# Gate stage: VectorE picks the two best experts of a chunk ahead of the low halves of the rows of the next one

## The reference

```python
logits = xf @ gate_w.T
topk_logits, topk_idx = jax.lax.top_k(logits, 2)
topk_w = jax.nn.softmax(topk_logits, axis=-1)
...
shared = jax.nn.silu(xf @ sg_gate.T) * (xf @ sg_up.T) @ sg_down.T
return shared + out
```

## Time and profile before

| | us |
|---|---|
| median of 3 timed runs | 2417.37 (2417.35 to 2419.74) |
| the profiled execution, its own time | 2425.1 |
| its span, first to last instruction | 2423.4 |
| VectorE busy in the span | 1776.7 |
| TensorE matmuls busy in the span | 2185.1 |

### The profile page before, as it was taken

One profiled execution on the slowest core, in us unless ns is written; L12 is line 12 of the kernel. 1 busy time (PEld: TensorE's weight loads), 2 busy tenths in 40 slices (PEclk: granted clock), 3 DMA queues, 4 the chain that ended last, 5 costly groups with the idle time before them and its releaser, 6 DMA issues. The chain is left out here.

```text
span 2423.4 us, 85735 instructions
## 1 busy us (share of the span) xinstructions
PE 2185.1 (90%) x31693; PEld 1375.4 (57%) x31693; DVE 1776.7 (73%) x5603; ACT 1664.1 (69%) x3894; POOL 1076.6 (44%) x1374
## 2 busy tenths in 40 slices
PE   6979999999967788879999995996999999999766
PEld 4643444444435676768888884563455555555354
DVE  5538999999838677744454444984999999999298
ACT  6955899899843555424454443893799999999644
POOL 3533666666654566636666664562000000000076
PEclk9987999999979899989999998997899999999888
DMA  6552333333232566745553344874232222322242
GB/s 220 203 189 75 93 91 94 94 94 93 65 97 87 146 181 185 171 115 128 141 139 96 93 89 127 267 274 147 65 80 79 81 75 81 82 74 69 64 155 95
DMA packets 363746, 290.45 MB, mean 120 GB/s; under 512 B 228400, under 2 KB 296752, under 8 KB 363344
## 3 DMA queue, kind: packets, MB, share of 16 engines
q1 hardware_dynamic: 349616, 248.24, 37.0%
q0 software_dynamic: 12960, 35.60, 4.7%
q10 hardware_dynamic: 768, 1.12, 0.2%
HBM read 133.53 MB, written 123.69 MB: 106 GB/s over the span
## 5 line engine op out<-in xcount | busy, mean ns | idle before, releaser
L765 ACT ACTIVATE a_pr<-a_pst 128x384 f32<-128x384 f32 (+3 forms) x2176 | 909.2, 486 | 112.6 <-PE a_pst L804 87.3
L804 PE MATMUL a_psc<-a_ke,a_qe 52*64 52x192 f16 (+4 forms) x6144 | 632.4, 286 | 32.5 <-DMA a_ke<-mrow 29.7
L804 PE MATMUL a_pst<-a_qe,a_ke 49*64 49x384 f16 (+5 forms) x6144 | 579.4, 288 | 1.6 <-ACT a_pr L765 0.5
L717 DVE TENSOR_REDUCE a_mx<-a_psc 128x1 f32<-128x320 f32 (+1 forms) x1152 | 537.9, 528 | 44.7 <-PE a_psc L804 36.8
L866 PE MATMUL a_po<-a_pr,a_ve 128*17 128x128 f32 (+3 forms) x10496 | 563.5, 303 | 2.0 <-ACT a_pr L765 1.1
L712 DVE CUSTOM_DVE_ANT_0 a_cut<-a_psc,row_mask 128x320 bf16<-128x320 f32 (+1 forms) x1024 | 436.3, 472 | 51.8 <-PE a_psc L804 29.6
L804 PEld LDWEIGHTS a_pst<-a_qe,a_ke 53*64 53x64 f16 (+1 forms) x6144 | 241.3, 105 | 327.9 <-ACT a_pr L765 193.9
L683 POOL TENSOR_SCALAR_AFFINE_SELECT a_pr<-a_pr 128x512 f32<-128x512 f32 x448 | 276.2, 637 | 159.4 <-ACT a_pr L765 159.4
L804 PEld LDWEIGHTS a_psc<-a_ke,a_qe 52*64 52x64 f16 (+1 forms) x6144 | 262.8, 106 | 112.1 <-DVE a_mx L717 36.3
L866 PEld LDWEIGHTS a_po<-a_pr,a_ve 128*17 128x17 f32 x10496 | 193.9, 96 | 181.9 <-issue 50.5
L663 POOL TENSOR_SCALAR a_mneg<-a_mx 128x32 f16<-128x32 f32 x64 | 18.6, 290 | 626.9 <-DVE a_mx L721 584.7
(11 more groups left out here) (242 smaller groups left out, 4168.6 us busy)
## 6 DMA issues: line engine op xcount, KB each, us to landing
a_qe<-qx SPq DMA_DIRECT2D x378, 64.0 KB, 2.7
a_ke<-kx SPq DMA_DIRECT2D x378, 64.0 KB, 2.7
vx<-p_vst SPq DMA_DIRECT2D x32, 544.0 KB, 3.3
a_ve<-vx SPq DMA_DIRECT2D x64, 272.0 KB, 3.0
qx<-p_stg SPq DMA_DIRECT2D x64, 256.0 KB, 3.4
kx<-p_stg SPq DMA_DIRECT2D x64, 256.0 KB, 3.3
ox<-a_ost SPq DMA_DIRECT2D x256, 64.0 KB
x_res<-x SPq DMA_DIRECT2D x16, 512.0 KB, 8.9
```

The lines of the kernel that those rows point to most:

```text
L717: dve.tensor_reduce(out.unsqueeze(1), psc[(u * n_s + n) % RING][:, 0:width], AXX, ALU.max)\
L765: act.activation(pr[s % SLOTS][:, h // 2, h % 2, 0:width], pst[prob_slot(u, n) % RING][:, 0:width], ACT.Exp, scale=scale).then_inc(p_ready, 1)
L804: last = pe.matmul(out[at, col:col + count], stat[:, t * P + 64 * half:t * P + 64 * half + 64], mov[:, tok:tok + count], start=(k == 0), s ...
```

## The change

In VectorE's queue of the gate stage, `top2(s+1)` is issued ahead of `row_lo(s+2)` in each iteration. In the last iteration but one there is no `row_lo`; in the last, `table_of_tiles` stands in the place of `top2`, and there is no `row_lo` either. Nothing else differs.

```diff
                 if s > 0:
                     add_y(s - 1, 1)
                 low(s, 0)
-                if s + 2 < NC:
-                    row_lo(s + 2)
                 if s + 1 < NC:
                     top2(s + 1)
                 else:
                     table_of_tiles()
+                if s + 2 < NC:
+                    row_lo(s + 2)
                 hidden(s, 1)
```

## The result

The changed kernel ran at a median of 2398.07 us (2395.67 to 2402.32, 4 runs), the kernel before on the same chip at 2418.34 us (2417.35 to 2419.74, 4 runs): a ratio of 0.9918, with a 95% interval of 0.9904 to 0.9932. Measured again on another chip, the ratio was 0.9911 (0.9894 to 0.9929). The number was right; the step of the working that gave it, the loop that sets the pace, was not.

The account below looks back on a forecast made before the run. VectorE's wait for ScalarE bounded the 15.84 us pace; afterwards the loop through the transposes would, at 14.3 us. Saving 17 us over 11 iterations plus about 1.5 in iteration 0, taken as 18 off 2417.4, gave 2399 us; range 2386 to 2417.

Parts of the forecast that it names:

- The hole (2.35 us): VectorE's wait before `row_lo` for ScalarE's L1300; `top2` (2.64 us) was to fit there, making all behind 2.35 us early.
- The delay behind the gates: In profiled iteration 14, gate completion reached VectorE 2.3 us after the last matmul began; assumed absent from timed runs.
- no change: Rival: delay behind the gates real in timed runs, transposes 8 us; pace 15.3 us, about 2414 us; chance 0.18.
- slower: Rival: delay behind the gates real, transposes 9.1 us; transpose loop 16.4 us against 15.84, total 2428 us; chance 0.10.
- The pace of 14.3 us from the loop through the transposes: Forecast case: gates, `top2`, `row_lo`, transposes (9.1 us), next gates set iterations 1 to 11 at 14.3 us; chance 0.44.
- the signs named ahead: Steady gates waiting for transposes, new wait before L1356, pace near 14.3 us; no DMA wait would mean transposes mis-sized.
- VectorE's own loop at 13.5 us: Rival: transposes 8 us or below, VectorE sets the pace, 15.84 less 2.35; 2388 or 2382 us; chance 0.20.
- Iterations 12 and 13: Gate-stage iterations without weight halves, already at 14.1 us with a wait for transposes; predicted to win nothing.
- The sum of 18 us: Predicted total gain: 17 us from iterations 1 to 11 and about 1.5 us from iteration 0.
- GpSimd's wait for slots: GpSimd's wait per iteration for VectorE's slots; predicted to fall from 3.2 to under 2 us.
- The rule on shared ports: VectorE instructions with two SBUF inputs and GpSimd's SBUF readers exclude each other; by it `row_lo` would take 1.23 us.

## Why the prediction was right or wrong

**The hole (2.35 us).** Right. `row_lo` stands right behind `top2`, without a wait for L1300. In the old order with block 0 on VectorE the instructions of an iteration take less time, and VectorE still waits there (1.38 or 2.02 us), so that the hole was a matter of order.

**The delay behind the gates.** The choice to put it down to the recording was right: a second profile of the unchanged kernel, and both profiles of the changed one, don't have it. Where VectorE does wait for the gates in the second profile of the changed kernel, `top2` starts 0.20 us after the last of them began (983.71):

```profile
983.91 0.19 DVE L1356 TENSOR_SCALAR g_logit<-g_small 128x32 f32<-128x32 f32 x1 [0.37 <-PE g_small L71]
```

The rivals "no change" and "slower" both hung on it, and fell with it.

**The pace of 14.3 us from the loop through the transposes.** This is the step that failed, though it came within 0.1 us of the measured 14.20. The loop is real, as the runs with extra transposes show, but it was mis-sized. Its main term was 9.1 us for the transposes, where at most 7.5 are measured at 891.89 to 899.36, 7.2 to 7.9 in the three chunks of the changed kernel whose gates waited, and 6.5 to 8.5 in the run with one transpose more. Two more terms were off and nearly made up for each other: `row_lo` took 1.13 us for 1.65, and `top2` 3.49 for 2.64. With the terms as measured (1.24 from `row_lo` to the first transpose, 7.4 to the gates, 0.7 for the gates, 0.2 to `top2`, and 3.49) the loop is at most 13.0 us long, under the 14.2 of VectorE's own. The 9.1 came from the one iteration where gates had waited, so from a slow case. The second profile of the kernel before has one too, in another iteration and of 9.8 us. The argument that a faster pace would crowd the DMA engines further did not hold for the landing times, although their share did rise from 0.67 to 0.76. By the signs named ahead, no steady wait of the gates for DMA meant exactly this, and the new wait before L1356 is missing from the steady iterations too.

**VectorE's own loop at 13.5 us.** This rival had the mechanism, and its price was wrong as well. 13.5 us was the old iteration less the hole, with every duration kept. The prediction knew that `row_lo` lost half a microsecond to L1270, and said that it "may go or come back elsewhere". It went, 0.52 us, and 1.33 us came back at two other places (`top2` 0.85, `low` 0.48), which makes 14.3 and, with 0.1 less in all the rest, the measured 14.2. With L1270 taken away the pace is 12.96 us (`top2` -0.86, weight half -0.55, `low` of half 1 -0.13, the third block of half 0 +0.33), so VectorE's own loop without collisions is shorter than either figure. Two errors, 9.1 for at most 7.5 in one loop and 13.5 for 14.2 in the other, met at nearly the same number. That the forecast of 2399 us lies so near the measured 2398 is luck: the loop that it was worked out from did not set the pace.

**Iterations 12 and 13.** The prediction gave them nothing, on the ground that they already wait for transposes. The last interval gave 1.8 us (14.10 to 12.30). VectorE's own row there had shown what it could give, a wait of 1.84 us for L1300 at 1010.67. The sum of 18 us was short by this, by 1 us in the eleven steady intervals (18.0 where the prediction had 17), and by half a microsecond of its own rounding (17 and 1.5 make 18.5). The profile shows 21.3, the timed runs about 20.

**GpSimd's wait for slots.** It was to fall from 3.2 to under 2 us and fell to 2.3. Its work per iteration shrank too (12.6 to 11.9 us), as the scatter beside `row_lo` is no longer stretched (1.79 us in the earlier trace rows, 1.02 at 905.88 here):

```profile
905.88 1.02 POOL L1264 DMA_INDIRECT xs<-g_xrow,g_slot  x1 [0.30 <-issue]
```

**The rule on shared ports.** L1373, L1377 and L1409, all with two inputs in SBUF, get longer beside L1270, and with L1270 elsewhere or gone they are short: that much the runs show. The Trainium skill (SBUF — State Buffer, section "Who interferes with whom") says that such instructions exclude each other for their whole length. The trace agrees in kind. In size it doesn't quite: the two instructions of `top2` lost 0.94 us beside an L1270 of 0.67. Nor in order, by the record, since L1373 began 0.66 us before L1270. The record of GpSimd's spans may be too rough to settle either.

## What to carry to other kernels

An empty stretch on the engine that sets the pace can be filled by moving work of that engine into it, if what it needs is there by then; after that, compare all loops that pass through the moved work, not only the old one. Moving a step shifts every later instruction against the other engines, so a collision seen at one place has to be priced at the new place too, or avoided: here a small instruction of GpSimd cost VectorE more than doing the work itself. A duration taken from the one place where somebody waited can be a slow case and not the usual one, as it was here; places that didn't wait bound it from above.

## What was not expected

- A transpose of half the size (128 by 256) takes SyncE 1.18 to 1.25 us to issue, a whole one (128 by 512) about 1.29 (5.16 us for four). So of these two sizes the smaller is hardly cheaper to issue.
- Four transposes landed sooner at the faster pace (within 7.5 us at a DMA share of 0.76) than in the kernel before in its one wait (9.1 us at 0.67). So the mean share alone doesn't tell how soon a transpose lands; what does was not tried.
- One profile can hold a delay that the next one of the same kernel, at the same pace, doesn't have: 2.33 us from the last gate matmul to `top2` in one, 0.90 in the other.
- Of the 22 us by which the changed kernel reached the first matmul of the routed experts earlier than the second profile of the kernel before (1035.81 against 1057.93), 19 were left at the end of the span (2400.6 against 2419.7). Where the 3 us go was not followed.
